# One language-model block in fp32: ScalarE instead of VectorE normalises the rows of the next groups in the attention stage

## The reference, cut to what matters

```python
h = base_weight[x] + einsum('bsr,dr->bsd', lora_A.T[x], lora_B)        # (64, 128, 512)
h = h + attn(layernorm(h))
h = h + ffn(layernorm(h))

def layernorm(x, eps=1e-5):
    m = mean(x, -1); v = var(x, -1)
    return (x - m) / sqrt(v + eps)

def attn(x):                                     # 16 heads of 32
    cq  = layernorm(x @ W_dq)  * q_g  + q_b      # 512 -> 128
    ckv = layernorm(x @ W_dkv) * kv_g + kv_b     # 512 -> 128
    Q = cq @ W_uq;  K, V = split(ckv @ W_ukv)
    o = softmax(causal(Q K^T / sqrt(32))) V
    return o @ W_o.T

def ffn(x):                                      # shared path and 16 experts, 8 of them chosen per token
    ...
```

## Time and profile before

| | us |
|---|---|
| median of 3 runs (2489.65, 2489.7, 2502.24) | 2489.7 |
| time of the profiled execution | 2494.0 |
| its span, first to last instruction | 2492.2 |
| TensorE busy in the span | 2366.0 (95%) |
| VectorE busy | 1786.4 (72%) |
| ScalarE busy | 1863.0 (75%) |
| GpSimd busy | 1179.5 (47%) |

### The profile page before, as it was taken

One profiled execution on the slowest core, in us unless ns is written; L12 is line 12 of the kernel. 1 busy time (PEld: TensorE's weight loads), 2 busy tenths in 40 slices (PEclk: granted clock), 3 DMA queues, 4 the chain that ended last, 5 costly groups with the idle time before them and its releaser, 6 DMA issues.

```text
span 2492.2 us, 47182 instructions
## 1 busy us (share of the span) xinstructions
PE 2366.0 (95%) x13379; PEld 1857.0 (75%) x13380; DVE 1786.4 (72%) x3651; ACT 1863.0 (75%) x4624; POOL 1179.5 (47%) x1333
## 2 busy tenths in 40 slices
PE   3799999999999999999999999999999999999998
PEld 2577667776777766688888888888888888888887
DVE  5788888888888885856656656656656656657655
ACT  1688888888888897867767767767767767767766
POOL 3454455555454442534534544544544544545544
PEclk9899999999999999999999999999999999999999
DMA  3222222222222223331321321321321321321322
GB/s 109 59 80 70 74 82 70 72 77 72 79 83 81 73 69 103 123 107 43 106 89 42 106 89 42 106 88 43 106 89 42 106 88 43 106 87 44 105 72 60
DMA packets 99829, 198.22 MB, mean 80 GB/s; under 512 B 10928, under 2 KB 10928, under 8 KB 99568
## 3 DMA queue, kind: packets, MB, share of 16 engines
q1 hardware_dynamic: 94576, 179.29, 22.1%
q0 software_dynamic: 5120, 17.31, 2.9%
HBM read 145.66 MB, written 50.86 MB: 79 GB/s over the span
## 4 chain that ended last, share of the span: by engine, by line
issue 30%; POOL 26%; PE 2%; DVE 1%; ACT 1%; POOLq 1%; DVEq 0%; ACTq 0%
POOL t_lo L1314 24%; POOL sh_lo L1314 2%; POOLq L1312 1%; DVE ps_u L1681 0%; DVE f_lo L1706 0%; DVE t L1688 0%; ACT t_hi L1533 0%; PE fwork L1329 0%; PE ps_g L1329 0%; ACT square L1516 0%; PE ps_g L1331 0%; PE ps_g L1330 0%; PE ps_u L1331 0%; PE ps_u L1329 0%; PE ps_u L1330 0%
## 5 line engine op out<-in xcount | busy, mean ns | idle before, releaser
L1314 POOL TENSOR_TENSOR t_lo<-t,t_hi 128x512 fp32r<-128x512 f32 x512 | 663.4, 1296 | 414.1 <-ACT t_hi L1533 414.0
L1681 DVE TENSOR_TENSOR ps_u<-ps_u,square 128x512 f32<-128x512 f32 x512 | 357.3, 698 | 155.2 <-ACT square L1520 140.0
L470 POOL TENSOR_TENSOR probs<-probs,inv 128x512 f32<-128x512 f32 x256 | 269.5, 1053 | 396.7 <-DVE inv L919 396.3
L1533 ACT ACTIVATE t_hi<-t 128x512 fp32r<-128x512 f32 x512 | 320.5, 626 | 111.1 <-PE ps_y L1331 65.7
L1688 DVE TENSOR_TENSOR t<-ps_u,res 128x512 f32<-128x512 f32 x512 | 354.1, 692 | 54.8 <-DVE ps_u L1681 20.5
L1516 ACT ACTIVATE square<-ps_g 128x512 f32<-128x512 f32 x544 | 320.1, 588 | 91.9 <-PE ps_g L1331 90.1
L732 ACT ACTIVATE probs<-ps_s,nmax 128x128 f32<-128x128 f32 x1024 | 368.6, 399 | 6.6 <-DVE nmax L909 3.9
L1520 ACT ACTIVATE square<-square 128x512 f32<-128x512 f32 x544 | 344.1, 633 | 17.3
L732 ACT ACTIVATION_READ_ACCUMULATOR probs<-ps_s,nmax 128x1 f32 x1024 | 244.4, 239 | 0.0
L1314 POOL TENSOR_TENSOR sh_lo<-t,sh_hi 128x512 fp32r<-128x512 f32 x32 | 42.0, 1313 | 389.6 <-ACT sh_hi L1533 389.6
L743 ACT ACTIVATE pT<-ps_t 128x512 f32<-128x512 f32 x256 | 158.8, 620 | 89.9 <-PE ps_t L625 88.7
(11 more groups left out here) (197 smaller groups left out, 5510.1 us busy)
## 6 DMA issues: line engine op xcount, KB each, us to landing
res<-w_rows SPq DMA_DIRECT2D x256, 256.0 KB, 3.2
h<-rows SPq DMA_DIRECT2D x64, 256.0 KB, 2.0
res<-h SPq DMA_DIRECT2D x64, 256.0 KB, 4.0
h<-res SPq DMA_DIRECT2D x64, 256.0 KB, 2.0
rows<-h SPq DMA_DIRECT2D x16, 1024.0 KB, 5.6
keep<-h SPq DMA_DIRECT2D x16, 1024.0 KB, 7.3
out<-keep SPq DMA_DIRECT2D x64, 256.0 KB, 2.3
keep<-in_w_ffn SPq DMA_DIRECT2D x12, 512.0 KB, 3.8
```

What stands on the lines that cost most here:

```text
L470: pool.tensor_tensor(probs[:, s % RING, :, :], probs[:, s % RING, :, :], inv[:, s % RING, :].rearrange("p (h o) -> p h o", o=1).to_broadca ...
L1314: pool.tensor_tensor(lo, t[:, t_slot(j), :], hi.bitcast(F32), ALU.subtract).then_inc(t_lo_done, 1)
L1533: act.activation(dst, t[:, t_slot(j), :], ACT.Copy).then_inc(t_hi_done, 1)
L1681: dve.tensor_tensor(dst, product, square[:, j % 2, :], ALU.mult).then_inc(t1_done, 1)
```

## The change

The subtraction and the multiplication become one ScalarE activation with a scale and a bias per row: `xn = rstd * h + shift`, with `shift = -mean * rstd`. GpSimd computes `shift` in step 7 behind the Newton rounds, two instructions of 128x4. ScalarE's four activations stand at the end of its step 10, behind the copy pT of slot 8. VectorE's four instructions go. Three waits come in: `h_add` and `c_seed` on VectorE and the shift on GpSimd wait for `xn_done`, since ScalarE now reads `h`, `nw` and `shift`.

```diff
+        shift = sb("row_shift", [P, TILES], F32)
...
+        shift_done = sem("row_shift_done")
...
                     if step == RSTD_AT and has_part(n, "xt", 0):
                         newton_of(2 * NEWTON_OPS * (n + 2), TILES)
+                        pool.wait_ge(newton, 2 * NEWTON_OPS * (n + 2) + NEWTON_OPS)
+                        at_least(pool, xn_done, TILES * (n + 2))
+                        shift_of(pool, shift_done, n + 2, moments[:, :, 0], nw[:, 4, 0:TILES], nw[:, 3, 0:TILES],
+                                 shift[:, :], pool_passed)
...
+            def normalise(g):
+                act.wait_ge(shift_done, 2 * (g + 1))
+                for t in range(TILES):
+                    act.activation(xn[:, t, :], h[:, t, :], ACT.Identity, scale=nw[:, 4, t:t + 1],
+                                   bias=shift[:, t:t + 1]).then_inc(xn_done, 1)
...
                     if not COPY_FIRST and has_slot(n, step - C_LAG):
                         pT_copy(n, step - C_LAG)
+                    if step == NORM_AT and has_part(n, "xt", 0):
+                        normalise(n + 2)
...
             def h_add(n, t):
                 full(dve, n, "h", t)
                 at_least(dve, res_kept[t], 16 * (n + 2))
+                at_least(dve, xn_done, TILES * (n + 2))
...
             def c_seed(g):
                 dve.wait_ge(c_moments, 2 * TILES * (g + 1))
+                dve.wait_ge(xn_done, TILES * (g + 1))
                 seed_of(2 * NEWTON_OPS * g + NEWTON_OPS, cmoments[:, :, 1], 2 * TILES)
-
-            def normalise(g):
-                dve.wait_ge(newton, 2 * NEWTON_OPS * g + NEWTON_OPS)
-                for t in range(TILES):
-                    dve.tensor_scalar(xn[:, t, :], h[:, t, :], moments[:, t, 0:1], nw[:, 4, t:t + 1],
-                                      ALU.subtract, ALU.mult).then_inc(xn_done, 1)
...
-                        if step == NORM_AT:
-                            normalise(n + 2)
```

## The result

The changed kernel takes 2486.5 us in the median of 17 executions (2484.6 to 2489.7); the kernel before, run beside it, takes 2489.7 (2486.8 to 2502.2). The ratio is 0.9969, with a 95% interval of 0.9954 to 0.9984: a gain that can be measured and that is less than the 0.5% which the forecast calls faster. Forecast were 2484.6 us and a range of 2474 to 2493. The ratio on record isn't the ratio of these two medians, which is 0.9987.

A forecast was written before the change was run, and what follows sets the result against it. VectorE's in-order queue was taken to bound k0's place in the attention stage, TensorE nearly all the rest. Turns -4.6 and start with turn 0 -0.5 gave -5.1 us from 2489.7: 2484.6, range 2474 to 2493.

The forecast's parts named there:

- The place and the size of the new gap: Before out3, turns 1 to 14: TensorE waits 1.3 to 1.6 us for ScalarE's k_diag copy; the wait before k0 goes.
- The price of the activation: Four normalisations in ScalarE's queue: 0.71 us each, 2.84 in all, taken from the same activation in the expert stage.
- The gain per turn: Attention stage: out3 starts at 457.60 instead of 457.93, so 0.33 us per turn, 4.6 us over 14 turns.
- the end of k0's copy: ScalarE's k0 copy, placed behind four exponentials ending at 456.93, takes 0.60 and ends at 457.53; out3 waits for it.
- The slow turns: Turns with TensorE's clock lowered behind the gap, 1.6 us each: three of 14 before, three assumed again, net 0.
- the carried difference: Profiled execution before, 2494.0, lies 4.3 us above the median; this was carried over to the changed kernel, giving base 2489.7.
- slower: the clock: Rival: the clock falls in more than three turns, 1.6 us each, up to 2502.2; chance 0.08 for above 2490.
- Start and turn 0: Before the steady turns: start gains net 0.9 us, low parts 1.5 earlier; turn 0 loses 0.4; together -0.5.
- GpSimd: Its two shift instructions in step 7 cost 0.7 us, covered by 0.9 before slot 7's transposes: cost nothing.
- The whole stall: Rival: k0's bank isn't late through ScalarE, TensorE keeps 1.68 x 14 = 23.5 us, total 2465.7; chance 0.08.
- Nothing is gained: Rival: ScalarE's four activations don't overlap, 0.80 us each, gain 0 per turn, about 2489 us; chance 0.17.
- ScalarE's instructions: Rival: the normalisations are as slow on ScalarE as they were on VectorE, total 2516 us; chance 0.02.

The follow-up runs named there:

- e1: The changed kernel with each of ScalarE's four normalisations cut into two halves of 256 columns: 2527.2 us, ratio 1.012 to the kernel before.
- e2: The changed kernel with all four head copies of k0 on VectorE, none on ScalarE: 2475.4 us, ratio 0.9916 to the kernel before.
- e3: The changed kernel with ScalarE's four normalisations one step later, behind its k0 copy: 2492.5 us, ratio 0.9991 to the kernel before.
- e9: The changed kernel with one of ScalarE's four normalisations, tile 0, cut into two halves: 2505.6 us, ratio 1.0039 to the kernel before.
- e5: The kernel before, VectorE still normalising, with all four head copies of k0 on VectorE: 2509.5 us, ratio 1.0052 to the kernel before.
- e6: The kernel before with GpSimd's two shift instructions added and nothing that uses them: 2502.2 us, ratio 1.0018 to the kernel before.
- e7: The kernel before with the change in turns -2 and -1 only, VectorE normalising afterwards: 2501.8 us, ratio 1.0028 to the kernel before.
- e10: The changed kernel run again unaltered, beside the variant with one tile in halves: 2486.5 us, ratio 0.9969 to the kernel before.

## Why the prediction was right, and where it wasn't

**The place and the size of the new gap: right.** k0's gap is gone, a new one stands before out3, released by ScalarE's k_diag copy, in 14 turns, 1.43 us long (forecast 1.3 to 1.6). e1 and e2 show that this copy is the cause.

**The price of the activation: right.** Four take 2.82 us of queue (forecast 2.84), each at a distance of 0.705; the row taken from the expert stage carried over unchanged to four in a row. Of the 59 in the trace between 100 and 900 us, 55 take 800 to 808 ns; the first four, in turn 0 (114.4 to 116.5), take 914 to 929, and no run shows why:

```profile
L702 ACT ACTIVATE keep<-rows,row_shift,nw x59: 800/803/929, 114.4 to 899.4; 128x512 f32<-128x512 f32 x59
```

The Trainium skill gives nearly the same by another way (ScalarE: Activation LUTs, What ACT_TABLE_LOAD costs): 186 ns, 0.833 a column and 93 for each pointer operand make an estimate of 799 for 512 columns, and an overlap of 93 makes 706. The rows agree, 803 and 705.

**The gain per turn: 0.23 for 0.33.** The term that was too large is the end of k0's copy. I set it right behind the exponentials; the last of these starts at 453.97, its successor would follow 0.345 later, at 454.32, and the copy starts at 454.46. That is 0.14 us, seen again in e3, where it follows the exponentials too: 458.65 for 458.15 + 0.345 = 458.50. The normalisations and the hand-over to TensorE (0.05 for 0.07) were each 0.02 shorter than forecast, and so 0.10 of the 0.33 is missing. Over 14 turns 3.2 us came for the 4.6 forecast.

The trace of the kernel before had the rows for this. Where its product is there already, a copy to k_diag starts 0.01 to 0.03 us after the end of ScalarE's previous instruction, and three in a row are 0.60 apart; a pT copy overlaps what is beside it:

```profile
436.62 1.79 ACT L719 ACTIVATE k_diag<-work 32x512 f32<-32x512 f32 x3
...
441.58 0.25 ACT L732 ACTIVATION_READ_ACCUMULATOR probs<-ps_s,nmax 128x1 f32 x1
441.86 0.59 ACT L719 ACTIVATE k_diag<-work 32x512 f32<-32x512 f32 x1
```

**The slow turns: the step that failed.** "I take three again: 0." In the profiled pair it was three against none, worth 4.8 us, more than all that the turns themselves gained. My reason was that a gap of nearly the same length stays. The table shows how much the little difference does. With gaps of 1.20, 1.26 and 1.43 us not one of 12 turns was slow, in four profiled executions; with 1.67 to 1.71 it was 2, 9, 11, 11 and 8 of 12, and 9 with 2.53. e9 has the changed kernel's order and engines, and with one tile in halves and a gap as long as the old one the slow turns are back. In the kernel before, e5, e6 and e7 nothing is halved and they are there too, so the length is what all these kernels share. It isn't all that decides: in one session all 12 executions of e9 lie above 2500 us, and 5 of 23 of the kernel before with a gap as long. What decides in one turn and not in the next at 1.7 us, these runs don't show: the kernel before ranges from 2486.8 to 2511.6 with the same code. The rival "slower: the clock" had the right mechanism and the wrong sign. As for its sign, the forecast did name the other way (4.8 us for no slow turn), but gave it no weight in the sum.

**Why the total still came out near.** 2484.6 was forecast and 2486.5 measured: the turns gave 1.4 us less than thought. The clock term that I left out is there in the profiled execution, which held three slow turns. The median of the kernel before lies 4.3 us lower, about the price of three slow turns, so it must hold fewer. I carried that difference over as if it belonged to both kernels. It doesn't: of the changed kernel the profiled execution (2484.6) lies 1.9 us under the median. Between the two profiled executions the forecast was -5.1 and -9.4 was measured; the carried difference was 4.3 and would have had to be -1.9. Errors of 4.3 one way and 6.2 the other left 1.9. Between the medians the account is plain: 14 x 0.23 = 3.2 us measured, 4.6 + 0.5 forecast. That forecast and profiled execution are both 2484.6 is chance.

**Start and turn 0: the part is right, the effect not to be seen.** The low parts come 1.51 us sooner after the seed in the profile (forecast 1.5), and turn 0's transposes wait for pT of ScalarE, 1.18 us, where they waited 2.15 for GpSimd. The mark in turn 1 came at 136.4 before, and at 135.0 and 138.7 in the two profiles of the changed kernel. Between 60 and 134 us the granted clock was 0.85, 0.91 and 0.83 in these three, so half a microsecond can't be read there.

**GpSimd: right.** 0.72 us for 0.7, covered, by e6. **Three waits: right**, no row of the waits names them.

**The rivals.** The whole stall doesn't go (e2 shows what it takes). "Nothing is gained" is excluded by turns of 56.16. ScalarE's instructions aren't slow.

## What to carry over

When a stall on a queue goes, follow the freed resource to its next user and to every engine that must release it; here a bank had two readers, and the second engine had been given the work that was taken from the first. A move between engines and a move of the last reader belong together: alone they were worth 0.23 and -0.49 us a turn, together 1.12. And where TensorE's clock falls in some turns of the profile, count these turns and price them before the edit is called neutral: a gap longer by a quarter of a microsecond came with 19 us more in this kernel (e9 against e10).

## What the hardware showed beyond that

- The granted clock falls for about 3 us behind a gap, while TensorE is working again and not while it waits: in e9 it is 1.00 in the gap from 402.92 to 404.62 and 0.50 from 405.05 to 408.40. The first matmul behind the gap takes 0.49 us, later ones 0.63. The matmuls' distance goes from 0.23 us to 0.43, near the ratio of 2.4 to 1.2 GHz. A turn of e9 pays 1.55 us.
- GpSimd got faster once VectorE's normalisations were gone. Of the 28 instructions that make cT_lo, two a turn, 14 took 1296 to 1300 ns before and the other 14, behind them, 1467 to 1484 (the median of 1384 lies between the two groups); now all take 1294 to 1304. Rows of the kernel before and of the changed one, 160 to 910 us, and the pair in one turn:

```profile
L476 POOL TENSOR_TENSOR cT_lo<-cT,cT_hi x28: 1296/1384/1484, 167.3 to 905.1; 128x512 fp32r<-128x512 f32 x28
...
449.26 2.73 POOL L476 TENSOR_TENSOR cT_lo<-cT,cT_hi 128x512 fp32r<-128x512 f32 x2
```

```profile
L478 POOL TENSOR_TENSOR cT_lo<-cT,cT_hi x28: 1294/1296/1304, 165.9 to 895.8; 128x512 fp32r<-128x512 f32 x28
...
446.66 2.56 POOL L478 TENSOR_TENSOR cT_lo<-cT,cT_hi 128x512 fp32r<-128x512 f32 x2
```

  All kernels that normalise on VectorE have the slower group, and none that normalises on ScalarE. In the turn of the earlier trace rows the four normalisations take 1544, 1508, 1257 and 534 ns; the first three start beside a large instruction of GpSimd and the last does not. So this is the contention that made the same work 0.53 us at best and 1.26 in the median on VectorE, seen from the other side. In the changed kernel's attention stage ScalarE's normalisations start behind the cT_lo pair and hardly test it. The expert stage does: all 60 of its normalisations run beside a large GpSimd instruction, take 798 to 806 ns, and the GpSimd instructions beside them take the usual 1292 to 1312. One of them, beside the row of 1044.22:

```profile
1044.40 1.29 POOL L1314 TENSOR_TENSOR t_lo<-t,t_hi 128x512 fp32r<-128x512 f32 x1 [1.34 <-ACT t_hi L1533]
```

  This agrees with the Trainium skill (SBUF — State Buffer, SBUF: two separate sides), by which VectorE and GpSimd share a port pair and ScalarE has its own. For the kernel's time it was worth nothing, since GpSimd doesn't bound the stage.
- ScalarE's k_diag copy, 32x512, doesn't overlap its neighbours: behind an exponential with an accumulator read it starts 0.48 to 0.53 us after the exponential's start, before and in the changed kernel. Another exponential starts 0.34 to 0.36 after it and a pT copy 0.34, in over 100 cases each. What in the k_diag copy's form does it, no run shows.
